# A four-layer fp32 network on one core: attention outputs stored by pixel with running sums for their statistics, and the last layer's first loads issued during the layer before

## The reference, cut to what matters

```python
# layer 0: token mixing by a recurrence over 16-pixel chunks
def _ttt_linear(...):
    ...
    _, out = jax.lax.scan(step, (W1_0, b1_0), (chunk(XQ), chunk(XK), chunk(XV), eta...))
    return _ln(out, post_w, post_b, EPS_IN) @ o_w.T
x = x + _L0_conv_ref(_gn(x), ...)
# layers 1 and 3: a product in the Fourier domain
def _L1_conv_ref(x, w1, w2, b1, b2):
    spec = jnp.fft.rfft2(x, axes=(2, 3), norm='ortho')
    # complex product by w1, bias, relu, complex product by w2, bias: per group of 128 channels
    out_c = out_c * spec
    return jnp.fft.irfft2(out_c, s=(H, W), axes=(2, 3), norm='ortho')
x = x + _L1_conv_ref(_gn(x), ...)
x = x + _L2_conv_ref(_gn(x), ...)   # a gate per channel from block means
x = x + _L3_conv_ref(_gn(x), ...)
```

## Time and profile before

| | us |
|---|---|
| runs, three of them | 5461.24, 5464.71, 5465.51; median 5464.71 |
| the profiled execution's own time | 5460.91 |
| its span, first to last instruction | 5458.9 |
| `opening` | 0 to 61 |
| `project` | 61 to 1560 |
| scan loop and its last tiles | 1560 to 3761 |
| statistics and norm between the layers | 3761 to 3784 |
| `fourier_forth` | 3784 to 4628 |
| gate and norms | 4628 to 4652 |
| `fourier_back` | 4652 to 5459 |

### The profile page before, as it was taken

The page is one execution under the profiler, slowest core; times in us unless marked ns, Lnnn a source line. Parts: engine busy times, 40 slices in busy tenths (PEclk is TensorE's granted clock), DMA queues, the critical chain, the costliest instruction groups (busy, mean ns, idle before and its releaser), DMA issues. The chain is left out here.

```text
span 5458.9 us, 134572 instructions
## 1 busy us (share of the span) xinstructions
PE 5180.7 (95%) x44534; PEld 3979.9 (73%) x44534; DVE 4166.4 (76%) x14714; ACT 2608.8 (48%) x7573; POOL 2701.1 (49%) x4382
## 2 busy tenths in 40 slices
PE   6999999999979999999999999997999996899998
PEld 3444444444448888888888888886899986799998
DVE  6766667655668888888888888885888888566665
ACT  0111111111147777777777777773555554454444
POOL 1444444444446666666666666662444543333332
PEclk8999999999979999999999999998999998899999
DMA  5434444433334444444444444443122211222221
GB/s 209 165 123 161 147 145 158 135 125 122 112 103 124 128 127 127 128 129 127 127 127 128 127 128 128 127 127 133 75 84 95 79 80 50 90 95 81 90 82 78
DMA packets 599450, 644.80 MB, mean 118 GB/s; under 512 B 172981, under 2 KB 503101, under 8 KB 587869
## 3 DMA queue, kind: packets, MB, share of 16 engines
q1 hardware_dynamic: 440844, 491.84, 27.8%
q10 hardware_dynamic: 157904, 144.22, 7.9%
HBM read 357.96 MB, written 278.00 MB: 117 GB/s over the span
## 5 line engine op out<-in xcount | busy, mean ns | idle before, releaser
L1628 PE MATMUL proj_ps<-proj_w_sb,proj_h 128*128 128x512 f32 x3072 | 1346.4, 596 | 0.0
L1628 PEld LDWEIGHTS proj_ps<-proj_w_sb,proj_h 128*128 128x128 f32 x3072 | 577.0, 190 | 742.1 <-issue 723.2
L1506 DVE SCALAR_TENSOR_TENSOR proj_lin<-proj_ps,proj_rstd,proj_wbias_sb 128x512 f32<-128x512 f32 x384 | 283.2, 746 | 492.9 <-PE proj_ps L1628 487.0
L1913 POOL TENSOR_TENSOR scan_b_step<-scan_core,scan_rate_last 128x128 f32<-128x128 f32 x512 | 331.7, 648 | 593.9 <-DVE scan_core L2145 593.9
L2354 PE MATMUL scan_ps_y<-scan_o_t,proj_wo_sb 128*128 128x128 f32 x4096 | 566.2, 281 | 2.1 <-ACT scan_o_t L2009 2.1
L2354 PEld LDWEIGHTS scan_ps_y<-scan_o_t,proj_wo_sb 128*128 128x128 f32 x4096 | 496.7, 191 | 32.3 <-ACT scan_o_t L2009 2.6
L1421 POOL TENSOR_TENSOR proj_gk<-proj_rec,proj_gain_sb 128x256 f32<-128x256 f32 x256 | 181.2, 728 | 526.4 <-DVE proj_rec L1527 526.4
L1982 ACT ACTIVATE scan_square<-scan_ps_z 128x64 f32<-128x64 f32 x1024 | 219.0, 219 | 460.0 <-PE scan_ps_z L2273 456.4
L1415 POOL TENSOR_TENSOR proj_by_cos<-proj_lin,proj_rope 128x512 f32<-128x512 f32 x256 | 335.9, 1326 | 162.8 <-DVE proj_lin L1506 121.1
L2285 PE MATMUL scan_ps_w<-scan_step,scan_record 64*128 64x128 f32 x4088 | 354.0, 292 | 14.8 <-DVE scan_step L2150 14.0
L1975 ACT COPY scan_state_w<-scan_ps_w 128x512 f32<-128x512 f32 x480 | 278.8, 581 | 122.3 <-PE scan_ps_w L2285 121.3
(11 more groups left out here) (326 smaller groups left out, 13190.2 us busy)
## 6 DMA issues: line engine op xcount, KB each, us to landing
scan_record<-records SPq DMA_DIRECT2D x259, 392.0 KB
records<-proj_rec ACTq DMA_DIRECT2D x256, 392.0 KB, 3.7
spectra<-fourier_spec SPq DMA_DIRECT2D x16, 2112.0 KB, 6.4
fourier_spec<-spectra SPq DMA_DIRECT2D x16, 2112.0 KB, 8.5
proj_h<-x SPq DMA_DIRECT2D x32, 1024.0 KB, 6.7
queries<-proj_q ACTq DMA_DIRECT2D x128, 256.0 KB, 3.9
gradients<-scan_stored SPq DMA_DIRECT2D x512, 64.0 KB
scan_q_in<-queries SPq DMA_DIRECT2D x128, 256.0 KB, 7.8
```

The lines of the kernel that those rows point to most:

```text
L1506: v.scalar_tensor_tensor(lin[q][:, n], ps[q][n][:], rstd[k][:, j:j + 1], T.wbias[:, n], ALU.mult, ALU.add).then_inc(lin_sb.sem, 1)
L1628: last = pe.matmul(ps[j % 2][n][:], h[k][:, ct, j * P:(j + 1) * P], T.w[:, n, ct], start=ct == 0, stop=ct == CT - 1)
L1913: v.tensor_tensor(b_step[g][:], core[g][:], rate_last[g][:, :, 2:3].broadcast_to([P, PB, HD]), ALU.mult).then_inc(b_step_sb[g].sem, 1)
```

## The change

What it does:

- **Folding.** `wo_bias` and the scaling of `T.wo` in `opening` go; VectorE copies `post_w` and `post_b` to `T.post`. `outputs_turned` applies them instead: four ACTIVATEs of 128x128 with scale and bias in place of one copy of 128x512.
- **Output product.** The tile's block is now the loaded side and the weights the moving side: call n of `tile_project` is one matmul of 512 columns, and the one that adds `x`. The result has pixels on partitions. `leave` is one copy of 128x512. The tile goes to DRAM by pixels, and `x1` has the shape (image, pixel, channel).
- **Statistics.** ScalarE squares the tile (`output_tile_squares`, 128x512, even step, ahead of `state_out(0)`). VectorE's `totals` adds the tile and its squares to running sums in SBUF, two TENSOR_TENSORs of 128x512, in the place of the four BN_STATS. After the loop 32 matmuls of one column and three small VectorE instructions replace the BN_AGGRs.
- **Layer 1's rows.** Pixels are on partitions already, so the 128 transposes of a unit's rows (32 a unit, 8 batches of four) and their evacuations go; `rows` multiplies straight from the loaded tile. The load of a unit is now in pieces of 128 channels.
- **Layer 1's engines.** ScalarE makes the column copies into `spec` and `symmetric`; VectorE takes 13 of the large boxes in one run at the unit's start; the squares move from the column batches into chunks 0 to 3.
- **Layer 3's start.** `LastLayer` holds spectra, weights, matrices for layers 1 and 3; SyncE loads weights and matrices of layer 3 after unit 0 of layer 1, and its first two spectra as soon as the last statistics have read those tiles.

The diff, cut to its core:

```diff
# opening
-            dve.wait_ge(wo_folded, 1)
-            steps.then(dve, v.tensor_copy(T.wo_bias[:], ps_small[:, 2]))
-            for ct in range(CT):
-                steps.then(dve, v.tensor_scalar(T.wo[:, ct], T.wo[:, ct], vecs[:, 2, ct:ct + 1], None, ALU.mult))
+            steps.then(dve, v.tensor_copy(T.post[:], vecs[:, 2:4]))
+            dve.wait_ge(wo_in, 16)
# scan_and_read, SyncE
-                    sp.dma_start(o_view[:, b * CT:(b + 1) * CT, bass.ds(...)], y_sb[par][:, b * CT:(b + 1) * CT]).then_inc(y_gone[b].sem, 16)
+                    sp.dma_start(x_out[b, sc * P:(sc + 1) * P], y_sb[par][:, b]).then_inc(y_gone[b].sem, 16)
# ScalarE
-                a.copy(o_t[:], ps_turn[:]).then_inc(o_t_sb.sem, 1)
+                for ct in range(CT):
+                    done = a.activation(o_t[:, ct], ps_turn[:, ct], ACT.Identity, scale=T.post[:, 0, ct:ct + 1], bias=T.post[:, 1, ct:ct + 1])
+                done.then_inc(o_t_sb.sem, 1)
...
-                for n in range(CT):
-                    done = a.activation(y_sb[par][:, b * CT + n], ps_y[:, n], ACT.Identity, bias=T.wo_bias[:, n:n + 1])
+                if t >= 8:
+                    act.wait_ge(total_sb.sem, total_sb.at(t - 7, 0))
+                a.copy(y_sb[par][:, b], ps_y[:]).then_inc(y_done.sem, 1)
+
+            def output_tile_squares(tile):
+                act.wait_ge(y_done.sem, y_done.at(t, 1))
+                if t >= 2:
+                    act.wait_ge(total_sb.sem, total_sb.at(t - 1, 0))
+                a.activation(y_sq[t % 2][:], y_sb[par][:, b], ACT.Square).then_inc(y_sq_sb.sem, 1)
...
# VectorE
-            def moments(tile):
-                for n in range(CT):
-                    v.bn_stats(where, y_sb[par][:, b * CT + n]).then_inc(stats_sb.sem, 1)
+            def totals(tile):
+                dve.wait_ge(y_done.sem, y_done.at(t, 1))
+                v.tensor_tensor(total[:, b, 0], total[:, b, 0], y_sb[par][:, b], ALU.add).then_inc(total_sb.sem, 1)
+                dve.wait_ge(y_sq_sb.sem, y_sq_sb.at(t, 1))
+                v.tensor_tensor(total[:, b, 1], total[:, b, 1], y_sq[t % 2][:], ALU.add).then_inc(total_sb.sem, 1)
...
-            for u in range(UNITS):
-                v.bn_aggr(chan_stats[:, u, :], stats6[:, u].rearrange("p s e -> p (s e)"))
+            dve.wait_ge(means_ps.sem, means_ps.at(0, 1))
+            steps.then(dve, v.tensor_copy(chan_stats[:], now))
+            steps.then(dve, v.tensor_tensor(chan_mean_sq[:], chan_stats[:, :, 0], chan_stats[:, :, 0], ALU.mult))
+            steps.then(dve, v.tensor_tensor(chan_stats[:, :, 1], chan_stats[:, :, 1], chan_mean_sq[:], ALU.subtract))
# TensorE
-                for ct in range(CT):
-                    pe.matmul(ps_y[:, n], T.wo[:, ct, n * P:(n + 1) * P], o_t[:, ct], start=ct == 0, stop=False)
+                pe.matmul(ps_y[:], o_t[:, n], T.wo[:, n], start=n == 0, stop=n == CT - 1, skip_group_check=True)
...
+            for b in range(B):
+                for ct in range(CT):
+                    for e in range(2):
+                        done = pe.matmul(ps_y[:, n:n + 1], total[:, b, e, ct * P:(ct + 1) * P], mean_of[:], start=True, stop=True)
# fourier_forth, SyncE
-                sp.dma_start(xb[k][:], x_view[bass.ds(u, 1)].rearrange("o c n -> (o c) n")).then_inc(x_loaded[k].sem, 16)
+                sp.dma_start(xb[k][:], x_view[u // CT, :, :, u % CT * P:(u % CT + 1) * P]).then_inc(x_loaded[k].sem, 16)
...
+            def load_next(u, k, body):
+                sp.wait_ge(s_stored[k].sem, s_stored[k].at(UNITS // 2, 0))
+                sp.wait_ge(energy_sb.sem, energy_sb.at(body + 1, 0))
+                sp.wait_ge(box_sb.sem, box_sb.at(body + 1, 0))
+                sp.dma_start(spec[k][:].rearrange("p s e h -> p (s e h)"), s_out[u]).then_inc(N.s_loaded[k].sem, 16)
+            load_next(0, 0, UNITS - 1)
             store(UNITS - 1, 1, col_sb.at(UNITS, 1))
+            load_next(1, 1, UNITS)
# VectorE
-                for n, (s, m) in enumerate(slots):
-                    v.tensor_copy(spec[k][:, s:s + m]..., psD[n % 2][:, 0:m * P]).then_inc(col_sb.sem, 1)
-                    if n >= 2:
-                        box_of_last(u, 1 - k, boxed)
+                boxed = 13
+                for g in range(boxed):
+                    box_of_last(u, 1 - k, g)
# TensorE
-            def turn_rows(u, i, k):
-                transposes(u, ROW + i, [xb[k][:, (4 * i + j) * P:(4 * i + j + 1) * P] for j in range(4)])
+            def rows(u, t, k, i):
+                for j in range(4):
+                    done = pe.matmul(psD[t % 2][:, j * P:(j + 1) * P], xb[k][:, 4 * i + j], F1, start=True, stop=True)
+                done.then_inc(dft_ps.sem, 1)
```

More of the change, by code:

```diff
@@ L155, in sig @@
             return Signal(ctx, nc, f"{name}_{n}", per, credit)
-        xb = [sb(f"x{k}", [P, TOK]) for k in range(2)]
+        xb = [sb(f"x{k}", [P, TOK // P, P]) for k in range(2)]
         wt = sb("weights", [P, CT, 4, P])
@@ L163, in fourier_forth @@
         half = sb("half", [P, TOK])
-        spec = [sb(f"spec{k}", [P, SLOTS, 2, H]) for k in range(2)]
+        spec = N.spec
         xsum = sb("xsum", [P, SLOTS, H])
@@ L553, in transform_rows @@
                     pe.wait_ge(row_sb.sem, row_sb.at(u, NB1 + i - 1))
-                transforms(u, ROW + i, [(j * P, j, F1) for j in range(4)])
+                rows(u, ROW + i, k, i)
             def turn_columns(u, n):
@@ L611, in unit @@
                     mix1(u, k, ct, c)
-                    if not last:
-                        turn_rows(u, c, 1 - k)
                 for c in range(NCH):
@@ L744, in unit @@
                     load(u + 2, k)
-            load(0, 0)
-            load_weights(0)
-            sp.dma_start(mats[:], d["dft"].rearrange("n p m -> p n m")[:, 4:8, :]).then_inc(const_in.sem, 16)
-            sp.dma_start(ident[:], d["dft"][8]).then_inc(const_in.sem, 16)
-            load(1, 1)
-            for ct in range(1, CT):
-                load_weights(ct)
+            sp.sem_inc(begun, 1)
             for u in range(UNITS):
@@ L2095, in body @@
                         outputs_turned(proj)
+                    if gone:
+                        output_tile_squares(gone)
                 if scan:
@@ L2598, in __init__, with sb @@
         self.made = ctx.enter_context(semaphore(nc, "scan_made"))
+class LastLayer:
+    def __init__(self, ctx, nc):
+        def sb(n, shape):
+            return ctx.enter_context(nc.sbuf_tensor(f"last_{n}", shape, F32))
+        self.spec = [sb(f"spec{k}", [P, SLOTS, 2, H]) for k in range(2)]
+        self.wt = sb("weights", [P, CT, 4, P])
+        self.bias = sb("bias", [P, CT, 4])
+        self.mats = sb("mats", [P, 4, P])
+        self.ident = sb("ident", [P, P])
+        self.const_in = Signal(ctx, nc, "last_const_in")
+        self.s_loaded = [Signal(ctx, nc, f"last_s_loaded{k}", 16) for k in range(2)]
+        self.w_loaded = [Signal(ctx, nc, f"last_w_loaded{ct}") for ct in range(CT)]
 def network(nc, d, out):
@@ L2641, in network @@
         last_coefficients(nc, gmean, grstd, gstd, keep, rest, coef)
-        fourier_back(nc, "fourier3", spectra, out, d["f3_w"], d["f3_b"], d, coef)
+        fourier_back(nc, "fourier3", spectra, out, coef, N)
 def rope_table():
```

176 lines of the change are left out of this document (83 added, 93 removed).

## The result

The changed kernel took 5524.51 us (median of four, 5516.1 to 5528.5), the kernel before, on the same chip, 5464.61. The ratio is 1.011, 95% interval 1.0098 to 1.0122: slower by 60 us. The profiled execution took 5528.5, its span 5526.6, 67.7 longer than before's.

| stretch | before | after | change | forecast |
|---|---|---|---|---|
| start to the first matmul of `project` | 81.5 | 79.6 | -1.9 | -2 |
| first to last 512-column matmul of `project` | 1437.5 | 1457.7 | +20.2 | 0 |
| first to last `update` of the scan | 2140.5 | 2229.4 | +88.9 | +90 |
| last `update` to the first `hidden` of layer 1 | 133.2 | 137.1 | +3.9 | -3.5 |
| 15 units of layer 1 | 747.3 | 717.3 | -30.0 | -33 |

What follows compares the result with a forecast made beforehand. TensorE was taken as the bound, VectorE close behind. Terms -2 + 90 - 2.5 - 1 - 34 - 10.7 = +39.8 on 5460.91 gave 5500.7; with the runs' median 3.8 higher, 5503 was given, range 5404 to 5532.

Steps and rivals of the forecast that it cites:

- The deciding term: Scan, VectorE and GpSimd: two-source sums take turns with `stored` and `zgain`, making `step` 1.01 us late; +90 us.
- rival 1: Scan: sums do not meet GpSimd as placed; scan changes -17 to +15 us, kernel faster, 5398 to 5430; chance 0.33.
- rival 2: Scan: GpSimd goes first or holds longer; +193 us, kernel 5608, or 5583 by the whole-instruction form; chance 0.08.
- Rival 4: Scan: delay about half; the scan's loss and 50 us gained elsewhere cancel, 5454 to 5476, no change; chance 0.07.
- slack argument: Scan: `step`'s lateness costs only beyond the gap before TensorE's `update`, 0.15 us usable, 0.60 in every fourth tile.
- TensorE's own gain: Scan: each `tile_project` call 0.03 to 0.035 us shorter, 0.14 a tile, -17 us if nothing comes late.
- Opening: Block's end: VectorE's four scalings, 2.05 us, go and a copy of eight columns stays; -2 us.
- Statistics: After the scan: 64 one-column records and three small instructions replace BN_AGGRs of 14.22 us; -2.5 us.
- Layer 1's start: First load in 512-byte pieces costs +2 us, eight fewer transpose batches ahead of unit 0 return about 3; -1 us.
- Layer 1: Eight transpose batches fewer a unit, partly lost to a later `hidden`: 2.2 us a unit, -34 in all.
- variant 3: Layer 1 gives nothing because 13 boxes push `hidden` by 3 us a unit; 5527, within the forecast's 0.52 chance.
- Layer 3: Start: GpSimd's 10.82 us wait for weights and bias goes because they are already on the chip; -10.7 us.

Runs made afterwards that it cites:

- e1_no_sums: The changed kernel with VectorE's two running sums of each tile replaced by two MEMSETs of one column; 5413.28 us, ratio 0.9907.
- e2_one_source: The changed kernel with each 128x512 sum replaced by one BN_STATS of 128x512 over the same tile, one SBUF source; 5443.74 us, ratio 0.9965.
- e4_before_sums: The kernel before with its four BN_STATS of a tile replaced by two 128x512 additions to sums in SBUF; 5559.99 us, ratio 1.0175.
- g3_split_sums: The changed kernel with only the sum of the squares moved to the end of VectorE's odd step, behind weights; 5527.27 us, ratio 1.0118.
- g1_one_sum: The changed kernel with the sum of the tile replaced by a one-column MEMSET, the sum of the squares kept in place; 5464.12 us, ratio 1.0008.
- g2_sums_last: The changed kernel with both sums moved to the end of VectorE's odd step, behind group 1's work and weights; 5533.82 us, ratio 1.0127.

## Why the prediction was right, and where it was not

Predicted 5503 in 5404 to 5532, slower with 0.60; measured 5524.5. (The sum gives 5500.7 + 3.8 = 5504.5, and 5503 was written.)

- **The deciding term held, in size and in detail.** 0.69 and about 0.8 for the sums, `stored` 0.93, `zgain` 1.7 were the marks; 0.68 and 0.88, 0.92, 1.71 came. `step` was to be 1.01 late and was 4.57 - 3.61 = 0.96; +90 was forecast, +88.9 came (0.72 and 0.715 a tile in the middle). The last microsecond of that match is luck: kernels with the same scan code gave +83.1 to +88.9. e1_no_sums, e2_one_source and e4_before_sums show the cause, not only the size. Rivals 1, 2 and 4 are out. (Rival 4 was also put wrongly: by rival 1's own figures a delay of 0.68 uses up the 50 us gained elsewhere, which is two thirds of 1.01 and not half.) The Trainium skill ("SBUF — State Buffer", the term "shared port pair") has such a pair exclude each other for the whole instruction. The trace bears out the turns but not that length: the second sum lasts 0.88, not 0.40 + 0.69. The +168 that the prediction got by it hangs on a delay of 1.61; its own 3.05 less 1.37 is 1.68, which would be +178, and either is far from what came.
- **Its slack argument was cruder than its result.** "Lateness costs only beyond the slack" of one `update` gave the right sum for this place. g3_split_sums shows that the same reading fails at another: a gap in front of TensorE is no room when VectorE's list is as long as the period.
- **TensorE's own gain held too.** -17 stood for 0.14 a tile if nothing came late. In e1_no_sums each of the four calls of `tile_project` takes 0.035 us less from its start to the next instruction (1.175 for 1.210 in two of the places), 0.14 a tile, and a tile in the middle is 0.12 shorter, 16 us in 128. The whole loop is only 7.3 shorter, because its first 16 tiles took 257.1 us against 251.0, at a mean granted clock of 0.89 against 0.92.
- **Opening**: -1.9, as forecast. **Statistics**: from their first instruction to the norm's first 12.2 us pass instead of 14.8 (the 64 small records take 10.97, where the BN_AGGRs took 14.22), -2.6 against -2.5. **Layer 1's start**: from VectorE's first instruction of the block to TensorE's first, which waits for the load, 2.4 more than before, against +2; from there to the first `hidden` 2.9 less, against -3.
- **Behind the loop the sums cost again, and that was left out: +3.9 came where -3.5 stood.** The tail of the scan, from the last `update` to the first statistic, grew by 5.9 (70.3 to 76.2) and was costed at nothing. It is the sums, not ScalarE's new order: e1_no_sums has the four ACTIVATEs of `o_t` and the squares, and its tail is 70.0; e2_one_source has 72.8, g1_one_sum 71.6; and e4_before_sums, the kernel before with the sums alone, has 79.5. Their place matters too: with both at the end of the step (g2_sums_last) the tail is 71.0. The clock has a share: its mean over the tail is 0.96 in the changed kernel, 0.91 in e4_before_sums and 1.00 before, in e1_no_sums and in g2_sums_last, which makes at most some 3 us of the 5.9. The rest was not taken apart. Another 1.0 came between the norm and layer 1's block, also unforecast.
- **Layer 1**: -2.0 a unit against -2.2. `hidden`'s wait grew by 0.69 a unit (17.3 us in 15 times against 7.0) where 0.9 was taken; a new wait of TensorE for ScalarE's evacuation of the turned blocks (13.3 us in 30 times) stands where one of 6.4 in 15 for VectorE's copies went, so the 0.3 that was to come back became 0.46 more. Bounds and mechanism held; variant 3 is out.
- **Layer 3**: -10.7 forecast, -10.4 with the early loads alone, and 7.8 lost where they were undone. In the changed kernel layer 3's start gives 10.5 of the 13.3; the last unit of layer 1 gives 1.5, against 1 forecast, and 1.3 came behind it.
- **What was not forecast at all is `project`, +20.2**. On the profiled execution the sum gave 5500.7 and 5528.5 came: 20.2 of the 27.8 are `project`, 7.4 the stretch ahead of layer 1, 3.0 layer 1, and the other terms came out 2.7 better. It had been left out because no line of it changed. The next section shows what happened there; why is open.

## What to carry to other kernels

Before trading a one-source instruction on VectorE for a two-source one, write down what GpSimd runs beside it and behind it: here 79 of 96 us in the scan loop came from the taking of turns, and only 17 from length (80 and 27 of 107 by its middle). Then count the engine's whole round, not the gap behind one instruction; when the list is as long as the period, moving work within it gives nothing, and closing a hole can bring two instructions together that the hole had kept apart. A good part of a large change (here the early loads) is worth timing alone.
